# Order of GpSimd's DMA issues in a mixture-of-experts layer: the spare weights' loads moved a tile sooner and ahead of the adds

## What is computed

```python
E, H, I, TOPK = (16, 512, 352, 4)
xs = x[tok]                       # tokens sorted by expert
gate = ragged_dot(xs, swapaxes(gate_weight, 1, 2), group_sizes)
up = ragged_dot(xs, swapaxes(up_weight, 1, 2), group_sizes)
h_act = silu(gate) * up
down = ragged_dot(h_act, swapaxes(down_weight, 1, 2), group_sizes)
out = zeros.at[tok].add(down * w_sorted[:, None])
```

## Time and profile before

| | before |
|---|---|
| median of three timed executions | 2158.46 us |
| the profiled execution | 2163.69 us, span 2161.5 us |
| TensorE busy | 1973.5 us, 91% |
| GpSimd busy | 567.5 us, 26% |
| hardware queue q1 | 163.90 MB, 22.5% of 16 engines' span |
| software queue q0 | 23.10 MB, 5.6% |

### The profile page before, as it was taken

One profiled execution on the slowest core, in us unless ns is written; L12 is line 12 of the kernel. 1 busy time (PEld: TensorE's weight loads), 2 busy tenths in 40 slices (PEclk: granted clock), 3 DMA queues, 4 the chain that ended last, 5 costly groups with the idle time before them and its releaser, 6 DMA issues.

```text
span 2161.5 us, 38438 instructions
## 1 busy us (share of the span) xinstructions
PE 1973.5 (91%) x14580; PEld 1560.8 (72%) x14580; DVE 1061.3 (49%) x2477; ACT 889.4 (41%) x1819; POOL 567.5 (26%) x416
## 2 busy tenths in 40 slices
PE   6989999996997999986899999999999999798886
PEld 6977777885446878774587777999989999633333
DVE  5546666764114366688747777333234555410111
ACT  4346666532223455566655544422253232211110
POOL 3333332322342211000031110333241110145553
PEclk9999999998998999997999999999999999899998
DMA  3200010238355221141020000222220000468895
GB/s 125 77 25 29 14 42 5 70 126 310 71 88 126 76 83 55 66 157 44 5 72 34 29 15 3 89 62 58 68 77 24 29 28 2 169 193 258 264 279 154
DMA packets 67918, 189.22 MB, mean 88 GB/s; under 512 B 15114, under 2 KB 16366, under 8 KB 62510
## 3 DMA queue, kind: packets, MB, share of 16 engines
q1 hardware_dynamic: 50606, 163.90, 22.5%
q0 software_dynamic: 17152, 23.10, 5.6%
HBM read 224.56 MB, written 20.91 MB: 114 GB/s over the span
## 4 chain that ended last, share of the span: by engine, by line
PE 75%; DVE 8%; DMA 7%; ACT 4%; issue 3%; SPq 1%; POOL 1%; ACTq 0%; DVEq 0%; POOLq 0%
PE psum L106 16%; PE psum L109 15%; PE psum L107 15%; DMA l3f_weights<-in_l3f_gate_up_dram 4%; PE psum L1580 4%; PE psum L900 3%; PE psum L3610 3%; PE psum L3578 2%; PE psum L2801 2%; PE psum L3596 2%; PE psum L1607 2%; PE psum L926 2%; PE psum L2447 1%; PE psum L3032 1%; PE psum L139 1%
## 5 line engine op out<-in xcount | busy, mean ns | idle before, releaser
L1580 PE MATMUL psum<-l3f_weights,l3f_x_turned 128*64 (+1 forms) x768 | 131.0, 498 | 30.6 <-issue 16.6
L1580 PEld LDWEIGHTS psum<-l3f_weights,l3f_x_turned 128*64 128x64 f32 x768 | 58.1, 148 | 94.2 <-issue 72.3
L2238 ACT ACTIVATE l2x_probs<-psum,l2x_shift 100x361 f32<-100x361 f32 x128 | 70.2, 562 | 97.3 <-DVE l2x_shift L2293 97.3
L1875 POOL TENSOR_TENSOR l2x_ctx_lo<-l2x_ctx_raw,l2x_ctx_hi 128x1448 fp32r<-128x1448 f32 x8 | 26.4, 3297 | 314.9 <-ACT l2x_ctx_hi L1883 314.9
L1676 DVE TENSOR_TENSOR l3f_h<-l3f_silu,psum 128x352 f32<-128x352 f32 x24 | 12.5, 522 | 164.4 <-ACT l3f_silu L1662 156.0
L3749 ACT ACTIVATE l0x_probs<-l0x_probs,l0x_lowest 100x361 f32<-100x361 f32 x128 | 75.2, 588 | 42.1 <-DVE l0x_lowest L3918 42.1
L106 PE MATMUL psum<-xn_hi,l2f_w_gu_hi 128*128 128x400 f32 x256 | 88.6, 346 | 1.6 <-DVE xn_lo L192 1.3
L448 POOL TENSOR_TENSOR l2f_w_gu_lo<-l2f_raw_gu,l2f_w_gu_hi 128x512 fp32r<-128x512 f32 x32 | 43.0, 1357 | 174.2 <-ACT l2f_w_gu_hi L463 174.2
L107 PE MATMUL psum<-xn_lo,l2f_w_gu_hi 128*128 128x400 f32 x256 | 87.8, 343 | 0.0
L2476 ACT ACTIVATE ln_squares<-l1x_clipped,l1x_key_shift,l1x_key_scale 128x400 f32<-128x400 f32 (+1 forms) x96 | 62.3, 712 | 51.4 <-DVE l1x_clipped L2515 51.4
L3918 DVE CUSTOM_DVE_ANT_0 l0x_probs<-psum,l0x_outside 100x361 f32<-100x361 f32 x128 | 62.9, 531 | 32.1 <-PE psum L3578 29.6
(11 more groups left out here) (553 smaller groups left out, 6120.9 us busy)
## 6 DMA issues: line engine op xcount, KB each, us to landing
l3f_weights<-in_l3f_gate_up_dram SPq DMA_DIRECT2D x24, 1408.0 KB
l3f_weights<-in_l3f_down_dram SPq DMA_DIRECT2D x24, 768.0 KB
l0x_w_raw<-in_slabs_dram SPq DMA_DIRECT2D x52, 256.0 KB, 2.6
l0f_weights<-in_slabs_dram SPq DMA_DIRECT2D x8, 1536.0 KB
l1x_piece<-in_bit_w_dram SPq DMA_DIRECT2D x8, 1024.0 KB, 6.4
l1f_raw<-in_bit_w_dram SPq DMA_DIRECT2D x8, 1024.0 KB, 8.3
l2f_raw_gu<-in_slabs_dram SPq DMA_DIRECT2D x32, 256.0 KB, 2.6
l0x_ctx_raw<-in_ctx_dram SPq DMA_DIRECT2D x8, 724.0 KB, 4.2
```

The source lines that it names most:

```text
L1580: mm = pe.matmul(c.psum[lanes, bank + x, 0:self.INNER], self.x_turned[:, t % 2, k, lanes], weights, start=k == 0, stop=k == KD - 1)
L1875: pool.tensor_tensor(self.ctx_lo[:, q, :, :], self.ctx_raw[:, :, :], self.ctx_hi[:, q, :, :], ALU.subtract).then_inc(self.s("ctx_split"), 1)
L2238: act.activation(self.probs[:, m % 2, g, :], c.psum[0:S, g, 0:C], ACT.Exp, bias=self.shift[:, g:g + 1], scale=self.SCALE, accum_out=self.t ...
```

## The change

In `pool`, GpSimd's program of this part, the order of issues is altered; no DMA is added or removed. Before the loop the gate and up part of the spare load of tile 1 is issued too. In turn t the gate and up part is that of tile t + 2 instead of t + 1, and it stands first; its wait is for gate_up(t), where the load of tile t + 1 waited for gate_up(t-1). The gather of tile t + 2 stands behind it as before. The down part of tile t + 1, which waits for down(t-1), now stands ahead of the adds of tile t - 1 instead of behind them. SyncE's program is not altered.

```diff
         self.gather(c, pool, 0)
         self.load_spare(c, pool, 0, 0)
+        self.load_spare(c, pool, 1, 0)
         self.gather(c, pool, 1)
         self.load_spare(c, pool, 0, 1)
         for t in range(self.TILES):
+            if t + 2 < self.TILES:
+                self.load_spare(c, pool, t + 2, 0)
+                self.gather(c, pool, t + 2)
             if t + 1 < self.TILES:
-                self.load_spare(c, pool, t + 1, 0)
-            if t + 2 < self.TILES:
-                self.gather(c, pool, t + 2)
+                self.load_spare(c, pool, t + 1, 1)
             if t:
                 self.add_up(c, pool, t - 1)
-            if t + 1 < self.TILES:
-                self.load_spare(c, pool, t + 1, 1)
         self.add_up(c, pool, self.TILES - 1)
```

## The result

The changed kernel takes 2129.32 us (median of 4 runs, 2128.21 to 2138.52), the kernel before 2157.99 us (4 runs, 2157.01 to 2158.97). The ratio is 0.9874, 95% interval 0.9851 to 0.9897: 27 us faster, 22 to 32. The forecast was 10.7 us and a range down to 2140.5 us. The profiled execution of the changed kernel took 2128.21 us, its span 2126.0 us.

The account below looks back on a forecast made before the run. Bound: a two-tile loop through the ring's load, lengthened by an empty spare load behind the adds. Terms: 8.6 + 4.1 (clock) - 1.0 (down part) - 1.0 (fuller engines) = 10.7 us, from 2158.46 to 2147.8 us; range 2140.5 to 2155.5.

Parts of the forecast that it names:

- What bounds the kernel, and the wait that goes: Last stage, two-tile loop: TensorE's gate and up waits for an empty spare load behind the adds; removing this wins 8.6 us.
- 11.64 - 10 x 0.30 = 8.6: Gain in us: ten waits between the ring's landing and TensorE's start, less 0.30 us each to start; ends 3.4 and 10.3.
- The down part ahead of the adds: GpSimd's software queue: the down part's burst meets the start of the ring's load, 0.1 us lost ten times, 1.0 us.
- The DMA engines get fuller: Last stage: busy share rises from 0.86 to 0.94, the ring's load lands later, 0.1 us lost ten times, 1.0 us.
- tile of 9.7 us: Time per tile assumed after the change, at which the DMA engines would be 0.94 busy.
- 201 us for 20 tiles: Sign of being right: the stage from tile 3 to tile 23 takes about 201 us, against 211.7 before.
- The clock: Gate and up of some tiles ran partly at 1.2 GHz after idle time; shorter waits win 4.1 us, ends 0 and 7.9.
- The clock did not stay as it was: Rival: TensorE's clock falls as often as before, leaving 6.6 us of gain, 2151.9 us; chance 0.24.
- nothing was given back: Rival: the ring's load lands later by the gain, or the gap was TensorE's own; 2157.5 us, chance 0.13.
- the gather never came late: Rival: the gather, now behind a wait for gate_up(t), lands late and TensorE stands; 17 us slower, 2175.8 us, chance 0.05.
- the prediction's 3 us: Upper end of the loss from the down part's packets at the ring's load, if DMA engines take even turns between queues.

Follow-up runs that it names:

- e3: Kernel before without any spare loads and without TensorE's waits for them: 2142.09 us, ratio 0.9926.
- e2: Kernel before with only the spare load's down part moved ahead of the adds, gate and up part at its old place: 2156.45 us, ratio 0.9992.
- e8: Changed kernel with the adds held later still by a scratch write of 1200 columns: 2134.66 us, ratio 0.9883.
- e9: e3 plus the spare load's down part alone, issued ahead of the adds: 2132.12 us, ratio 0.9878.
- e13: e9 run again, on the same chip as e14 and e15: 2133.81 us, ratio 0.9872.
- e16: Changed kernel with the gather ahead of the spare load's gate and up part instead of behind it: 2131.25 us, ratio 0.9869.
- e1: Changed kernel with the spare load's down part put back behind the adds, so only the gate and up part comes sooner: 2138.23 us, ratio 0.9904.
- e15: e9 with the spare load's down part behind the adds instead of ahead: 2147.02 us, ratio 0.9939.
- e4: Kernel before with the adds held by a scratch write of 1200 columns on GpSimd: 2160.38 us, ratio 1.0001.
- e7: Kernel before with the adds held by a scratch write of 2200 columns on GpSimd: 2161.52 us, ratio 1.0017.
- e6: e3 (no spare loads) with the adds held by a scratch write of 2200 columns: 2140.0 us, ratio 0.9907.
- e14: e6 run again, on the same chip as e13: 2140.54 us, ratio 0.9905.
- e12: e1 with the adds held by a scratch write of 2200 columns: 2143.85 us, ratio 0.9925.

## Why the prediction was wrong

**What bounds the kernel, and the wait that goes: right.** The spare load behind the adds ended the wait. Without spare loads (e3) 16 us go, and in the changed kernel the time between landing and start is 0.19 us. The term "11.64 - 10 x 0.30 = 8.6" should have been 11.6 - 1.9 = 9.7 us.

**"The down part ahead of the adds", 1.0 us lost: the step that failed.** Its bounds were 3 us lost to 3 us won, from the length of the burst, as if the burst's own packets were all that counts. (The burst was misread too: rows 7 have six slices above nothing, 0.2 us and not 0.3.) What the runs show instead is that the place of the empty load in its queue moves the landing of the ring's load, in the other queue. With the down part ahead of the adds the landing is 9.5 to 9.9 us after the down product in all kernels that have it so (changed, e2, e8, e9, e13, e16), and 10.0 to 10.7 us in all that have it behind or not at all (the two groups nearly touch, at e2 and e1). In time it is worth 13 us (e13 against e15, one chip), 10 us (e9 against e3) and some 6 us (changed against e1), the last two across chips. It looked as if it worked by holding back the adds, 2 KB packets that run in the last microseconds of the ring's load in the kernel before; that alone is not it, as the last paragraph of this section shows.

**"The DMA engines get fuller", 1.0 us lost: wrong sign.** The landing got shorter although the engines went from 0.86 to 0.97 busy. The step's own tile of 9.7 us did not fit the forecast either, whose 201 us for 20 tiles are 10.05 us each. Together with the step above it makes 1.2 us per loop won instead of 0.2 lost, over ten loops 14 us, the larger part of the miss. By e1, 0.7 of the 1.2 us come without the down part ahead of the adds; why the landing is that much shorter there is not shown.

**The clock: 4.1 us forecast, 7.9 measured in the two traces.** The mechanism held. Gate and up of tiles 4, 8, 10 and 19 were 7.9 us too long; in the changed kernel each of tiles 4 to 23 takes 4.95 to 4.96 us:

```profile
1957.08 4.95 PE L1580 MATMUL psum<-l3f_weights,l3f_x_turned 128*64 x32 [0.52 <-issue]
...
2058.03 4.95 PE L1580 MATMUL psum<-l3f_weights,l3f_x_turned 128*64 x32 [1.30 <-issue]
```

No idle time there is over 1.30 us. I had taken two thirds of the three clearest tiles; all three and tile 19 came back, and with them tile 23's, outside the stretch (7.33 us before, 4.95 after). That the term is as large as 7.9 us is in part luck of the trace before, since e4 and e7 have one or two such tiles and not four.

The sum by measured terms: 9.7 + 11.7 + 7.9 = 29.3 us, against 29.9 in the two traces. The 11.7 are ten times the landing's 1.17 us. The medians differ by 28.7 us, and by 26.5 us on the second chip.

**The rivals.** The clock did not stay as it was, nothing was given back, and the gather never came late: TensorE did not wait ahead of line 1589 in the stretch. The rule of the Trainium skill that I weighed ("DMA: Bandwidth & Descriptors", "Queues, rings and completion order": turns between the queues) pointed at a loss from small packets ahead of the ring's load. In the changed kernel the down part is issued 0.8 us after the down product, and its packets run from some 5 us after it on, at the tail of the ring's load, not at its start. By the same section of the Trainium skill a packet is typically 9 to 17 descriptors. If the profile's 144 packets of 4 bytes, nine to an engine, are single descriptors, they are about one turn and not nine, and the prediction's 3 us do not follow from the rule. The measurement decides: no loss was seen.

**What stays open.** Why the last count comes so much sooner. In e6 and e9 the software queue holds about the same share of the engines from 6 to 8 us after the down product (8% each), and still the landings differ by 0.5 us. The first packets of the adds come at 7.4 us in e6 and 7.5 in e14, at 7.6 in e9 and e13 (medians): nearly the same. In e7 the share is 6% and in e12 4%, with the adds from 7.5 and 7.7 us on, and the ring's load still lands at 10.2 and 10.3 us. So neither the adds' first packet nor the share of the queue sets the landing; the place of the empty load does, and how is not shown. A kernel with the scratch and the empty load ahead of the adds, and neither of the other loads, was not run.

## What to carry to other kernels

When a wait is for a transfer that moves nothing, look at what stands ahead of it in its queue, and issue it before the slow ones. When a DMA is moved within a queue, cost not only its own packets but also those behind it, and ask which other queue's load is under way at that moment. And test the two halves of an edit both alone and together: here one half was worth nothing without the other.

## What was not expected of the hardware

An indirect DMA of 128 rows, all out of bounds, put ahead of two accumulating DMAs made a 1.4 MB load in another queue land 0.6 us sooner (9.8 against 10.4 us, e13 and e15), with nothing else in the program changed. The adds, issued 1.0 us after the down product in the kernel before, start to run 6.5 us after it (median of 18 tiles); behind the empty load 7.6 to 7.8 us after it, and held by a scratch write alone 7.4 to 7.5 us. And the DMA engines, which seemed short of time at 0.86 busy, moved 304 GB/s at 0.97 in the same stage where they had moved 265.
